# Transposing two row tiles of a fused attention and expert kernel by DMA instead of TensorE, and adding a constant row by VectorE instead of by DMA

## The chip, the cores and the metric

The kernel runs on the 8 cores of one Trainium2 chip. Each core works on one sequence of 4096 rows by 1024 columns and talks to no other core. The metric is the device time of the slowest core, in microseconds. Before the change it is 1058.75 us (median of 3 runs, 1055.48 to 1062.07).

Each core has engines that run their own instruction streams and meet at semaphores: TensorE (PE, matmul), VectorE (DVE), ScalarE (ACT), GpSimd (POOL), and SyncE (SP), which here only issues DMA. POOL issues DMA too, through another queue; both queues share 16 DMA engines.

## The reference, cut to what matters

```python
# per core: x [4096, 1024]; 16 heads of 64; chunks of 128 rows
q, k, v = phi(x @ Wq.T + bq), phi(x @ Wk.T + bk), x @ Wv.T + bv     # phi = elu + 1
for each chunk i:                                     # per head, state S, z carried along
    scores = tril(q_i @ k_i.T)
    out_i  = (scores @ v_i + q_i @ S) / sum(q_i * (cumsum(k_i) + z))
    S, z   = S + k_i.T @ v_i, z + sum(k_i)
x = layernorm(x + out @ Wo.T + bo)
gates = softmax(x @ gate_w.T + gate_b); top 2 of 8 experts per row
x = layernorm(x + sum over the two of gate * (x @ expert_w[e].T + expert_b[e]))
```

## The kernel before

The first stage (about 50 to 650 us) goes over the sequence in 32 chunks of 128 rows; the second (from about 655 us) over 39 tiles of rows sorted by expert, twice. The change touches the first stage only.

Every engine's stream is written out in program order; an engine runs its own rows strictly in that order and stops at the first wait that isn't met. One pass g of the chunk loop writes, in this order, work on three or four chunks at once:

- the norm of chunk g-2 (`stage_ln`, two ACT instructions), writing `x1b` (bf16 rows) and `xf` (f32 rows), and the top-2 gating of chunk g-3 (`stage_top2`, eight small DVE instructions, the sixth of which gives the one-hot tile `oh`);
- chunk g's key transposes and scores on PE (`stage_kt`, `stage_scores`). DVE copies the keys out of PSUM (L417) and masks the scores in two halves (L438);
- one "unit" (`nxt()`), which is 8 matmuls of 128x512 for the projections of the next 512 columns of the sequence. A query or key unit is drained by two ACT instructions (L325, L326) and one DVE instruction (L330), a value unit by one ACT instruction (L339). Then the rank matmuls of chunk g-3 (`stage_rank`, L656 and L658), which wait for `oh`;
- `stage_attnT(g - 1)`: 8 PE transposes of the attention rows `attn` into PSUM (L529) and an ACT copy to `attnT` (L535); a unit; `stage_x1T(g - 2)`: the same for `x1b` into `x1T` (L593, L599);
- `stage_numden(g)`: 24 small matmuls (L461, L467). Those of a half need that half of the masked scores. DVE divides and writes `attn` (L479, L483);
- a unit, the state update (`stage_state`), the output projection of chunk g-1 (`stage_oproj`, L547, from `attnT`), whose DVE part adds the residual rows `x0b` (L554) and takes the norm's statistics; a unit; the gate matmuls of chunk g-2 (`stage_gate`, L609, from `x1T`); two more units.

A pass has six units once the first four chunks are through. In passes 4n to 4n+2 the last two are key or query units, so DVE's last instruction of the pass is L330; in passes 4n+3 the last two are value units and DVE has nothing of them. Units stop with pass 30; passes 28 to 31 have few.

The residual rows plus a constant row `cbc` (bo plus bv times Wo) are made by DMA alone: SP copies `cbc` into `x0b(g)` inside SBUF (`preset_x0`), and POOL then issues a DMA of x with `accum_op=add` onto it (`add_x0`). `x0b(g)` is free again when chunk g-2's L554 is done. `cbc` itself is made in pass 0 by `make_c` (c_tok).

## Time and profile before

| | |
|---|---|
| median of 3 runs | 1058.75 us (1055.48 to 1062.07) |
| profiled execution, its own time | 1057.53 us |
| its span on the slowest core (core 6) | 1056.0 us; the other cores 1041.1 to 1051.1 |
| busy over the span | PE 908.1 us (86%), DVE 576.9 (55%), ACT 540.7 (51%), POOL 431.5 (41%) |
| middle of the chunk loop, 101.9 to 594.8 us (492.9 us) | PE 462.4 us, DVE 331.7, ACT 312.4, POOL 191.3 |
| DMA, share of 16 engines | POOL's queue 54.9%, SP's queue 26.3% |

The last but one line is the middle of the chunk loop, from pass 2 to pass 29. Busy time alone says that PE is nearest to full there, at 94%. What ends its idle time is read from the timeline of single passes, whose period is 17.3 to 19.0 us. Times in a timeline are those of the start; an instruction's duration overlaps the next one's start by 0.05 to 0.1 us on DVE and by more on PE, so what an instruction adds is best read as the difference of two starts.

### The profile page before, as it was taken

How to read it: one execution, taken by the hardware profiler on the slowest of the kernel's cores; microseconds unless marked ns; L12 is line 12 of the kernel's file. 1: busy time of each engine (PE TensorE's matmuls, PEld its weight loads, DVE VectorE, ACT ScalarE, POOL GpSimd, SP SyncE). 2: the span in 40 equal slices, each digit the busy share in tenths (PEclk: the TensorE clock that was granted, in tenths of full speed). 3: DMA queues.
4: the chain of work that ended last, by engine and by line, in shares of the span. 5: the costliest groups of instructions: out<-in, count | busy, mean ns of one | idle time of the engine just before them, and what ended most of it. 6: DMA issues, size and time to landing. Idle time of an engine off the chain costs nothing.

```text
span 1056.0 us, 21222 instructions; the slowest of 8 cores (1041.1 to 1056.0 us)
## 1 busy us (share of the span) xinstructions
PE 908.1 (86%) x6495; PEld 457.0 (43%) x6606; DVE 576.9 (55%) x1243; ACT 540.7 (51%) x731; POOL 431.5 (41%) x674
## 2 busy tenths in 40 slices
PE   4799899999998999999999863579778899999992
PEld 1344454555544545554555541234333344444441
DVE  4345766766666667666667764000000088888883
ACT  0663665756657566566656541112112455666552
POOL 9101433534434334325232424313222356777763
PEclk9899999999999999999999986889989899999997
DMA  9989796977976967868537995989999768987861
GB/s 139 160 156 314 138 209 143 177 156 149 180 155 130 189 150 137 189 126 157 137 106 226 285 294 180 296 160 235 182 168 255 203 210 277 309 267 249 304 208 58
DMA packets 126490, 204.96 MB, mean 194 GB/s; under 512 B 59422, under 2 KB 73886, under 8 KB 126384
## 3 DMA queue, kind: packets, MB, share of 16 engines
q0 software_dynamic: 53808, 130.92, 54.9%
q1 hardware_dynamic: 72576, 72.69, 26.3%
q8 instruction: 59, 0.97, 0.4%
q14 instruction: 47, 0.39, 0.1%
HBM read 142.93 MB, written 97.21 MB: 227 GB/s over the span
## 4 chain that ended last, share of the span: by engine, by line
PE 52%; ACT 11%; issue 10%; DMA 8%; POOL 7%; DVE 7%; SPq 3%; DVEq 0%; ACTq 0%; POOLq 0%
PE PS L309 20%; PE PS L960 13%; PE PS L547 10%; ACT AR L325 4%; DMA AR<-xs 4%; POOL out L206 3%; ACT AR L326 3%; DMA W<-wq 2%; SPq L983 2%; PE PS L467 1%; PE PS L593 1%; PE PS L461 1%; POOL rstd L1126 1%; DMA y2d<-AR,ix 1%; PE PS L502 1%
## 5 line engine op out<-in xcount | busy, mean ns | idle before, releaser
L309 PE MATMUL PS<-W 128*128 128x512 bf16 x1474 | 347.9, 384 | 33.6 <-DVE acc L266 15.0
L960 PE MATMUL PS<-W,AR 128*128 (+1 forms) x1215 | 285.3, 391 | 46.1 <-DMA AR<-xs 40.3
L309 PEld LDWEIGHTS PS<-W 128*128 128x128 bf16 x1536 | 143.7, 99 | 192.4 <-issue 38.4
L960 PEld LDWEIGHTS PS<-W,AR 128*128 128x128 bf16 x1248 | 121.6, 100 | 208.3 <-issue 80.8
L330 DVE SCALAR_TENSOR_TENSOR W<-AR 128x512 bf16<-128x512 f32 x128 | 88.5, 692 | 140.6 <-ACT AR L326 125.3
L325 ACT ACTIVATE AR<-PS,cbs 128x512 f32<-128x512 f32 x128 | 87.9, 687 | 87.8 <-PE PS L309 82.6
L547 PE MATMUL PS<-W 128*128 128x512 bf16 x496 | 115.2, 386 | 6.5 <-DVE ixf L637 3.2
L1022 ACT ACTIVATE AR<-PS 128x1024 f32<-128x1024 f32 x39 | 39.8, 1023 | 152.2 <-PE PS L960 147.3
L1066 DVE COPY wT<-PS 16x128 bf16<-16x128 bf16 x39 | 7.3, 188 | 186.5 <-PE PS L1058 186.0
L206 POOL DMA_INDIRECT xs<-AR x32 | 34.5, 1078 | 181.4 <-DVE rden L479 143.0
L1096 ACT ACTIVATE AR<-AR,nmr,rstd 128x1024 f32<-128x1024 f32 x39 | 48.4, 1241 | 80.4 <-POOL nmr L1129 80.4
L206 POOL DMA_INDIRECT y2d<-AR,ix x39 | 37.6, 963 | 125.0 <-ACT AR L1022 110.4
L326 ACT ACTIVATE AR<-PS,cbs 128x512 f32<-128x512 f32 x128 | 87.7, 685 | 0.0
L438 DVE TENSOR_TENSOR W<-PS,cbs 128x1024 bf16<-128x1024 f32 x64 | 75.1, 1215 | 0.1
L547 PEld LDWEIGHTS PS<-W 128*128 128x128 bf16 x512 | 48.3, 99 | 60.6 <-issue 8.1
L518 ACT ACTIVATE AR<-S_f 64x520 bf16<-64x520 f32 x62 | 39.8, 642 | 51.1 <-DVE S_f L509 46.6
L206 POOL DMA_INDIRECT out<-AR x39 | 53.1, 1360 | 30.2 <-issue 9.9
L565 POOL TENSOR_TENSOR rstd<-mnv,epst 128x1 f32<-128x1 f32 x32 | 6.2, 194 | 137.5 <-DVE mnv L563 120.4
L1111 DVE SCALAR_TENSOR_TENSOR AR<-PS,AR 128x1024 f32<-128x1024 f32 x39 | 50.1, 1284 | 21.3 <-PE PS L960 20.9
L402 POOL DMA_DIRECT2D AR<-x x32 | 32.3, 1046 | 67.6 <-DMA AR<-AR 67.3
L1117 DVE BATCH_NORM_STATS2 lnst<-AR 128x6 f32<-128x512 f32 x78 | 50.2, 685 | 6.5 <-DVE AR L1111 6.2
L1107 DVE SCALAR_TENSOR_TENSOR AR<-AR 128x1024 f32<-128x1024 f32 x39 | 50.1, 1285 | 4.7 <-DMA AR<-y2d,AR 3.6
(123 smaller groups left out, 1265.4 us busy)
## 6 DMA issues: line engine op xcount, KB each, us to landing
AR<-xfd SPq DMA_DIRECT2D x39, 524.0 KB
AR<-AR SPq DMA_DIRECT2D x32, 512.0 KB, 5.8
AR<-x POOLq DMA_DIRECT2D x32, 512.0 KB, 7.2
escr<-ew POOLq DMA_DIRECT2D x64, 256.0 KB
W<-escr SPq DMA_DIRECT2D x40, 256.0 KB, 5.1
W<-xt POOLq DMA_DIRECT2D x64, 128.0 KB, 12.7
W<-escr SPq DMA_DIRECT2D x48, 128.0 KB
xfd<-AR SPq DMA_DIRECT2D x9, 524.0 KB, 6.2
```

The source lines that it names most:

```text
L206: return Q.op("POOL", lambda e: e.indirect_dma_start(out=out, out_offset=bass.IndirectOffsetOnAxis(ap=idx, axis=0), in_=in_, in_offset=Non ...
L309: return Q.op("PE", lambda e: e.matmul(bank(b), lt, rh, start=(k == 0), stop=(k == KB - 1)), inc="cpe" if k == KB - 1 else None)
L325: Q.op("ACT", lambda e: e.activation(e1, bank(b), AF.Exp, bias=bc), inc="cac")
L326: va = Q.op("ACT", lambda e: e.activation(e2, bank(b), AF.Relu, bias=bc), inc="cac")
L330: vd = Q.op("DVE", lambda e: e.scalar_tensor_tensor(dst, e1, 1.0, e2, ALU.min, ALU.add), inc="cdv")
L438: msc_tok[j][hf] = Q.op("DVE", lambda e, hf=hf: e.tensor_tensor(msc[j][hf].rearrange("p (h w) -> p h w", w=128), PS[:, hf * 1024:(hf + 1) ...
L547: vpe = Q.op("PE", lambda e, b=b, k=k, hh=hh: e.matmul(bank(b), attnT[j][:, k * 128:(k + 1) * 128], wcol(3, k, hh * 512, 512), start=(k == ...
L960: mm = e.matmul(bank(2 * pi + hh), xTb[i][:, k * 128:(k + 1) * 128], w, start=(lst == 1 and k == 0), stop=(k == KB - 1))
L1096: vo = Q.op("ACT", lambda e, x=x, val=val: e.activation(val, val, AF.Identity, bias=nmr[x][:, 0:1], scale=rstd[x][:, 0:1]), inc="cac")
L1107: v1 = Q.op("DVE", lambda e, i=i, j=j, val=val: e.scalar_tensor_tensor(val, Y[j], XF[i][:, F_GATE + 1:F_GATE + 2], val, ALU.mult, ALU.add) ...
L1111: v2 = Q.op("DVE", lambda e, i=i, pi=pi, val=val: e.scalar_tensor_tensor(val, PS[:, pi * 1024:(pi + 1) * 1024], XF[i][:, F_GATE:F_GATE + 1 ...
L1117: vb = Q.op("DVE", lambda e, i=i, x=x, hh=hh: e.bn_stats(lnst[x][:, hh * 6:(hh + 1) * 6], XF[i][:, hh * 512:(hh + 1) * 512]), inc="cdv")
```

## The change

Two independent edits.

First, for the first 24 chunks the 8 PE transposes of `attn` and their ACT copy are left out, and so are those of `x1b`; in their place SP issues one DMA transpose each, from SBUF to SBUF (`move_attnT(g)` after `stage_numden(g)`, `move_x1T(g - 2)` after `stage_ln(g - 2)`). Chunks 24 to 31 keep the PE form.

Second, for all 32 chunks SP loads x plainly into `x0b` (`load_x0`), and DVE adds `cbc` with one 128x1024 f32 instruction (`add_c(g)`) at the end of pass g. The copy of `cbc` and POOL's accumulating DMA are gone.

```diff
+    def load_x0(g):
+        Q.wait("SP", *(et_free if own(g) else [x0_free[g % 2]]))
+        x0_tok[g] = dma("SP", f"dx{g % 2 + 2 * own(g)}", x0b(g),
+                        dx[g * 128:(g + 1) * 128, :])
+
+    def add_c(g):
+
+        Q.wait("DVE", x0_tok[g], c_tok[0])
+        x0_add[g] = Q.op("DVE", lambda e: e.tensor_tensor(x0b(g), x0b(g), cbc, ALU.add),
+                         inc="cdv")
+
+
+    moved = lambda g: g < NCH - 8
+
+    def turn(sem, out, in_):
+        return Q.op("SP", lambda e: e.dma_start_transpose(
+            out.rearrange("p (k m) -> p k m", m=128), in_), inc=sem, k=16)
+
+    def move_attnT(g):
+        j = g % 2
+        Q.wait("SP", attn_tok[j], attnT_free[j])
+        attnT_tok[j] = attn_free[j] = turn(f"dat{j}", attnT[j], attn[j])
+
+    def move_x1T(g):
+        x, j = g % 3, g % 2
+        Q.wait("SP", x1b_tok[g], x1T_free[j])
+        x1T_tok[g] = turn(f"dxT{j}", x1T[j], x1b[x][:, 0:1024])
+        x1b_free[x] = [x1T_tok[g]]
...
             stage_ln(g - 2)
+            if moved(g - 2):
+                move_x1T(g - 2)
             stage_meta(g - 2)
...
-        if on(1) and g < NCH:
+        if on(1) and g < NCH and not moved(g - 1):
             stage_attnT(g - 1)
         nxt()
         if late:
             nxt()
-        if on(2):
+        if on(2) and not moved(g - 2):
             stage_x1T(g - 2)
...
-        if on(0) and g > 0 and not own(g):
-            add_x0(g)
-        if g == NCH - 4:
-            add_x0(NCH - 2)
-            add_x0(NCH - 1)
         if on(0):
             stage_numden(g)
+            if moved(g):
+                move_attnT(g)
...
         if g == 0:
-            preset_x0(0)
-            add_x0(0)
+            load_x0(0)
+        if on(0):
+            add_c(g)
         if g + 1 < NCH - 2:
-            preset_x0(g + 1)
+            load_x0(g + 1)
         if g == NCH - 5:
-            preset_x0(NCH - 2)
-            preset_x0(NCH - 1)
+            load_x0(NCH - 2)
+            load_x0(NCH - 1)
```

On DVE, the end of a pass whose last units are query or key units and the top of the next pass read so before (L330 drains the units, L629 to L646 are the gating, L417 and L438 the copy of the keys and the mask):

```order
106 L330 SCALAR_TENSOR_TENSOR W<-AR 128x512 x2
107 L629 RECIPROCAL rg<-sg 128x1
108 L630 MAX t<-eg 128x8
109 L632 MAX_INDEX ix<-t,eg 128x8
110 L633 TENSOR_SCALAR AR<-t,rg 128x2
111 L637 CAST ixf<-ix 128x2
112 L639 TENSOR_TENSOR oh<-cbs,ixf 128x16
113 L646 TENSOR_TENSOR AR<-oh,t 128x16
114 L417 COPY AR<-PS 128x1024
115 L438 TENSOR_TENSOR W<-PS,cbs 128x1024 x2
```

In the changed kernel, whose lines are numbered 18 higher from there on, the same place reads:

```order
110 L330 SCALAR_TENSOR_TENSOR W<-AR 128x512 x2
111 L403 TENSOR_TENSOR AR<-AR 128x1024
112 L647 RECIPROCAL rg<-sg 128x1
113 L648 MAX t<-eg 128x8
114 L650 MAX_INDEX ix<-t,eg 128x8
115 L651 TENSOR_SCALAR AR<-t,rg 128x2
116 L655 CAST ixf<-ix 128x2
117 L657 TENSOR_TENSOR oh<-cbs,ixf 128x16
118 L664 TENSOR_TENSOR AR<-oh,t 128x16
119 L435 COPY AR<-PS 128x1024
120 L456 TENSOR_TENSOR W<-PS,cbs 128x1024 x2
```

The new row L403 stands between the drain of the last unit and the gating; everything behind it is in its old order.

On PE, between the gate matmuls of one pass and the first matmuls of the next pass's `stage_numden`, the rows were:

```order
224 L609 MATMUL PS<-gw_b,AR 128x8 x8
225 L309 MATMUL PS<-W 128x512 x16
226 L412 MATMUL PS<-id_b,W 128x128 x8
227 L433 MATMUL PS<-W 128x128 x16
228 L309 MATMUL PS<-W 128x512 x8
229 L656 MATMUL PS<-oh,stri_b 128x16
230 L658 MATMUL PS<-acc,ones_b 128x16
231 L529 MATMUL PS<-id_b,W 128x128 x8
232 L309 MATMUL PS<-W 128x512 x8
233 L593 MATMUL PS<-id_b,AR 128x128 x8
234 L461 MATMUL PS<-AR,W 128x130
```

and are now:

```order
209 L627 MATMUL PS<-gw_b,AR 128x8 x8
210 L309 MATMUL PS<-W 128x512 x16
211 L430 MATMUL PS<-id_b,W 128x128 x8
212 L451 MATMUL PS<-W 128x128 x16
213 L309 MATMUL PS<-W 128x512 x8
214 L674 MATMUL PS<-oh,stri_b 128x16
215 L676 MATMUL PS<-acc,ones_b 128x16
216 L309 MATMUL PS<-W 128x512 x8
217 L479 MATMUL PS<-AR,W 128x130
```

Both sets of 8 transposes (L529, L593) stood between the scores and `stage_numden`, and both are gone from there; nothing else on PE has moved.

## Rows read from the trace of the kernel before

**Rows 1.** Page, part 2: busy tenths of PE in 40 slices of the span
```profile
PE   4799899999998999999999863579778899999992
```
**Rows 2.** Stretches: us, busy (count) of PE, PEld, DVE, ACT, POOL; PEclk, DMA share, GB/s
```profile
101.90:594.80 492.90, 462.39 (x4057) 252.85 (x4122) 331.67 (x806) 312.39 (x473) 191.29 (x333) 1.00 0.76 163
198.60:215.90 17.30, 17.09 (x152) 9.42 (x154) 9.66 (x28) 10.17 (x16) 8.25 (x14) 1.00 1.00 188
```
**Rows 3.** Timeline, top of pass 10: start us, us, engine line operation [idle before <-releaser]
```profile
242.65 0.30 ACT L622 ACTIVATE eg<-lg,ngm 128x8 f32<-128x8 f32 x1 [1.23 <-DVE ngm L619]
245.22 1.25 ACT L579 ACTIVATE AR<-AR,nmr,rstd 128x1024 bf16<-128x1024 f32 x1
245.45 0.69 DVE L330 SCALAR_TENSOR_TENSOR W<-AR 128x512 bf16<-128x512 f32 x1 [0.47 <-ACT AR L326]
246.06 0.16 DVE L629 RECIPROCAL rg<-sg 128x1 f32<-128x1 f32 x1
247.32 0.17 PE L656 MATMUL PS<-oh,stri_b 128*128 128x16 bf16 x1 [0.78 <-DVE oh L639]
247.39 0.69 DVE L417 COPY AR<-PS 128x1024 bf16<-128x1024 bf16 x1
247.99 2.35 DVE L438 TENSOR_TENSOR W<-PS,cbs 128x1024 bf16<-128x1024 f32 x2
248.22 1.89 PE L309 MATMUL PS<-W 128*128 128x512 bf16 x8 [0.17 <-DVE AR L417]
249.95 0.61 PE L593 MATMUL PS<-id_b,AR 128*128 128x128 bf16 x8
250.39 0.22 PE L461 MATMUL PS<-AR,W 128*128 128x130 bf16 x1
251.56 1.67 PE L309 MATMUL PS<-W 128*128 128x512 bf16 x7
253.38 0.69 ACT L325 ACTIVATE AR<-PS,cbs 128x512 f32<-128x512 f32 x1 [1.67 <-PE PS L309]
258.73 0.34 PE L609 MATMUL PS<-gw_b,AR 128*128 128x8 bf16 x8
```
**Rows 4.** Timeline, top of pass 12, behind value units
```profile
280.08 0.16 DVE L619 TENSOR_REDUCE ngm<-lg 128x1 f32<-128x8 f32 x1
281.19 0.16 DVE L629 RECIPROCAL rg<-sg 128x1 f32<-128x1 f32 x1 [0.96 <-ACT eg L622]
283.14 2.35 DVE L438 TENSOR_TENSOR W<-PS,cbs 128x1024 bf16<-128x1024 f32 x2
286.28 0.61 PE L593 MATMUL PS<-id_b,AR 128*128 128x128 bf16 x8
```
**Rows 5.** Page, part 5: the nearest row to the new addition
```profile
L1107 DVE SCALAR_TENSOR_TENSOR AR<-AR 128x1024 f32<-128x1024 f32 x39 | 50.1, 1285 | 4.7 <-DMA AR<-y2d,AR 3.6
```
**Rows 6.** Timeline and chain of work that ended last, passes 0 to 2
```profile
83.71 1.19 SPq L194 DMA_DIRECT2D xfd<-AR  x1
...
85.42 6.64 DMA AR<-AR
...
87.74 0.69 DVE L330 SCALAR_TENSOR_TENSOR W<-AR 128x512 bf16<-128x512 f32 x1 [2.39 <-ACT AR L326]
88.35 0.68 DVE L417 COPY AR<-PS 128x1024 bf16<-128x1024 bf16 x1
...
100.88 0.69 DVE L554 TENSOR_TENSOR AR<-PS,AR 128x512 f32<-128x512 f32 x1 [4.09 <-DMA AR<-x]
101.93 1.67 PE L309 MATMUL PS<-W 128*128 128x512 bf16 x7 [1.31 <-DVE AR L554]
107.33 0.61 PE L593 MATMUL PS<-id_b,AR 128*128 128x128 bf16 x8 [1.56 <-ACT AR L579]
```
**Rows 7.** One line's instructions: count, duration ns min/median/max; and a stretch of the second stage
```profile
L983 SPq DMA_TRANSPOSE AR<-xs x39: 1237/1464/13554, 651.7 to 823.9; - x39
...
800.00:830.00 30.00, 29.89 (x137) 13.62 (x139) 0.00 (x0) 9.21 (x9) 9.63 (x10) 1.00 1.02 256
```
**Rows 8.** Timeline, top of pass 30
```profile
603.75 0.16 DVE L629 RECIPROCAL rg<-sg 128x1 f32<-128x1 f32 x1 [0.59 <-ACT eg L622]
```

More of the change, by code:

```diff
@@ L379, in build @@
     rden_tok = [None, None]
-    x0_set, x0_free = {}, [None, None]
+    x0_tok, x0_free = {}, [None, None]
     x0_add = {}
@@ L393, in build @@
     x0b = lambda g: tmp[:, g % 2 * 1024:(g % 2 + 1) * 1024] if own(g) else x0c[g % 2]
-    def preset_x0(g):
-        Q.wait("SP", *(et_free if own(g) else [x0_free[g % 2]]), c_tok[0])
-        x0_set[g] = dma("SP", f"dc{g % 2 + 2 * own(g)}", x0b(g), cbc)
-    def add_x0(g):
-        Q.wait("POOL", x0_set[g])
-        x0_add[g] = Q.op("POOL", lambda e: e.dma_start(
-            x0b(g), dx[g * 128:(g + 1) * 128, :], accum_op=ALU.add),
-            inc=f"dx{g % 2 + 2 * own(g)}", k=16)
+    def load_x0(g):
[19 more added lines that the diff above has]
+        x1b_free[x] = [x1T_tok[g]]
     def stage_kt(g):
```

## The prediction

> **What bounds the kernel now.** I read the page's busy slices first, then the stretches of the chunk loop, then the timeline of single passes. The slices show PE at eight tenths or more from the third to the 23rd slice [rows 1], and the middle of the chunk loop has PE busy 462.4 of 492.9 us, DVE 331.7, at full clock, with the DMA engines at 0.76 [rows 2]. So 30.5 us of PE time are idle there over some 27 passes. That looks like a loop bound by PE, from which any PE work taken out would be gained. The timeline says that this is only half true. At the top of pass 10 [rows 3] two chains run side by side from the pass before to `stage_numden`. PE's own: units, key transposes, scores, unit, rank, attnT, unit, x1T, numden. And one over ACT and DVE: the gating's exponential (L622) waits for DVE and delays the draining of the last units on ACT; DVE then drains the last unit (L330 at 245.45), runs the gating (from 246.06), copies the keys (247.39) and masks the scores (247.99, 2.35 us, done 250.34). PE waits for that chain twice, 0.78 us for `oh` before L656 and 0.17 us for the bank that L417 frees, and starts numden at 250.39, 0.05 us after the masks are done. The two chains are equally long; what is taken from PE alone between them gains little, and what is put on DVE there costs. Behind value units (pass 12, [rows 4]) DVE is ahead instead: it stands idle 0.96 us before L629, and its masks are done at 285.49, 1.24 us before numden (286.73, below). Passes with index 4n+1, 4n+2 and 4n+3 have the first form, passes 4n the second.
>
> **The change part by part.**
>
> *PE transposes out.* A set of 8 occupies PE from 249.95 to 250.39, 0.44 us [rows 3]. 24 sets of each kind are left out: 48 x 0.44 = 21 us is the most that PE alone could give back. The ACT copies go too, but behind them ACT stands idle waiting for PE before its next unit (1.67 us before 253.38, [rows 3]), so I cost them at nothing; what hides them is the next unit's matmuls.
>
> *The addition in.* No row has an f32 sum of two 128x1024 SBUF tiles. The nearest has the same size, type and two SBUF operands and takes 1.285 us [rows 5]; the masks, with one operand in PSUM, take 2.35 us for two. From those a start-to-start cost of 1.13 to 1.28 us; I take 1.15, since L438 starts follow each other about 1.13 apart. It is placed behind L330 and ahead of L629, so the whole gating, the key copy and the masks are queued behind it, and PE waits for `oh` and for the masks.
>
> *Pass of the first form, redone with both edits (pass 10).* L330 ends its turn at 246.06; the addition holds DVE to 247.21; `oh` and so L656 move from 247.32 to 248.47. The unit behind it no longer needs the transposes' bank and starts at 248.54, runs 1.73 (248.22 to 249.95, [rows 3]) to 250.27. The masks are done at 250.34 + 1.15 = 251.49, the first half near 250.36. numden's first half runs 250.45 to 250.9, its second must wait for 251.49, starts at 251.6 and ends at 252.05. Before, the unit behind numden started at 251.56 less its missing first record, about 251.35. **+0.72 us per pass**, although PE has 0.9 us less to do: PE now stands idle about 1.9 us for `oh` and 0.7 us for the second mask.
>
> *Pass of the second form (pass 12).* The addition starts at 280.2 in DVE's idle time and ends at 281.35, 0.15 us later than L629 started [rows 4]. The masks stay ahead of PE. Both sets of transposes are gained, 2 x 0.44, and the short wait at the scores with them: **-0.9 us**; numden began at 286.28 + 0.45 = 286.73 and would begin at 285.85.
>
> *Sum over the loop.* Both kinds are out in passes 4 to 24: 15 passes of the first form, 15 x 0.72 = +10.8, and 6 of the second, 6 x -0.9 = -5.4. Together +5.4 us.
>
> *Passes 25 to 31.* Pass 25 has one set back, +0.9. Passes 26 and 27 have both sets back and the addition, up to +1.0 each. In passes 28 to 31 DVE waits 0.59 us for ACT before L629 [rows 8], so 1.15 - 0.59 = 0.56 us is left: four times, 2.2. In all +5 us at most; I take 4.2, since pass 28 comes behind value units.
>
> *The start.* Before, the sum of x and the constant for chunk 0 was late: the copy was issued at 85.42 and took 6.64 us, the accumulating DMA came behind it, DVE waited 4.09 us at L554 and PE 1.31 and 1.56 us behind it [rows 6]. Now the load is issued behind SP's init rows (until 84.90) and the new transpose of chunk 0 (about 1.3 us, the issue time of the second stage's transposes, [rows 7]), so at 86.2, and if it takes the same 6.64 us it lands at 92.9. DVE comes to the addition at 88.35 and stops there, and behind it in its queue stand L417 (then at 88.35) and pass 1's masks, for which PE's numden of pass 1 waits. Masks and numden are late by 92.9 + 1.15 - 88.35 = 5.7 us; 2.87 us of PE waits that followed are gone. **+3 us** (0 if the load is quick, +5.7 if those waits stay).
>
> *The transposes by DMA.* Those of the second stage, from HBM, are 39, of the same 128x1024 bf16; SP spends 1.46 us on one at the median, and from 800 to 830, where PE has 137 matmuls, 16 to a tile, so a tile in 3.5 us, it is busy 29.89 of 30 us [rows 7]. So one costs at most 3.5 us of throughput. From SBUF none is in the trace; between 1.3 and 3.5 us is my bound if the source makes no difference. What hides them: `x1T` can be issued when L579 is done (246.47) and is needed at 258.73 [rows 3], 12.3 us; `attnT` has a whole pass, about 17. SP has two of them and a load in a pass of 18.6 us. In DMA time one copy and an accumulation of 512 KB go, a plain load of 512 KB and two transposes come: about 0.76 to 0.85 of the engines. I cost them at nothing. Without cover, each us that `x1T` is late costs a us.
>
> *POOL* loses 32 DMA issues of 1 us, and waits elsewhere: nothing.
>
> *Sum.* +5.4 + 4.2 + 3 = +12.6 us on the profiled execution's 1057.53 us (its span 1056.0 and 1.5 around it), 1070.1. The median of the runs is 1.2 us above that execution: **1071 us**.
>
> **The rivals.**
>
> *Faster.* The one way is that the addition finds a gap. The point from which it decides is DVE's cost of the addition: at 0.55 us or less a first-form pass gains nothing or better, and at zero the second half of numden starts right at 250.34 + 0.1 and ends at 250.9, -0.43 per pass. That gives 15 x -0.43 - 5.4 = -12, with the start at 0 to +3: 1047 to 1050. For it speaks that busy time has PE at 94%, and that ACT, freed of 2 us per pass, might drain earlier than I think; against it that DVE's L330 waits only 0.47 us before the addition's place and that ACT's delay there comes from L622, not from the copies. Chance 0.17.
>
> *x1T late.* Behind pass 4n+2 POOL issues eight loads of xt and three casts right before `x1T` is ready, and the stretch there has the DMA engines at 1.00 [rows 2]. A transpose shares the rings with them. If it takes over 12.3 us there, PE waits at the gate matmuls. Two us late in those six passes gives +12, 1083; one us in all 24, +24, 1095. For it: the longest issue of a transpose in the second stage, 13.55 us, behind other traffic [rows 7]. Against: PE lived with 1.02 of DMA share in 800:830 without a wait. Chance 0.2.
>
> *The transposes fill the queue.* If one from SBUF takes more than 18.6 / 2 = 9.3 us, two per pass are more than the pass. At the 13.55 us of the longest, 27.1 - 18.6 = 8.5 us per pass, 24 times: +204, far off. The 3.5 us speaks against it. Chance 0.05.
>
> A rule stands beside this one. The Trainium skill, page "VectorE: DVE Perf Modes", section "The three transpose paths", has 390 ns for a 128x128 block on TensorE and 1309 ns by DMA, and its rules say to use TensorE where PSUM will do, which speaks against the change. Eight blocks in a row would be an estimated 10.5 us by that page, two of them 21 us per pass, and the sum 2.4 x 24 = 58 us above the present time. The second stage's at most 3.5 us for eight blocks doesn't agree with taking them in a row; no run here shows it from SBUF.
>
> *Nothing moves*, gains and losses of the passes cancel at 1055 to 1062. Chance 0.08.
>
> **How the numbers follow.** My forecast has 0.5, own range 1062 to 1079: the addition at 1.13 to 1.28, the start 0 to 5.7, the late passes 2 to 5. Late x1T 0.2, full queue 0.05, faster 0.17, nothing 0.08. The range from 1049 to 1092 leaves out most of the full queue, a fifth of the late x1T, and half of the faster case. About 1% is what a measurement of this kernel can tell from no change, 1048 to 1069. Slower than that: 0.32 of my forecast, 0.2 and 0.05: 0.57. Within: 0.18, the 0.08 and 0.03 of the faster case: 0.29. Faster: 0.14.
>
> **What would show it.** Right: in first-form passes PE's wait before the rank matmuls (`oh`) grows from 0.8 to near 1.9 us, and a new wait for the masks of 0.5 to 0.8 us stands inside numden; periods of 19.4 us there and 16.5 in the fourth; no wait of PE for a DMA at the output projection or the gate; DVE idle before the first addition for about 4.6 us. Wrong: the addition far from 1.15 us; waits of the gate matmuls for `x1T`; or a DVE chain that has moved ahead as a whole, with all passes near 17.5 us.

## The result, and the profile after

The median of 4 runs of the changed kernel is 1095.5 us (1088.35 to 1104.58). Kernel before, run beside it on the same chip: 1058.75 us (3 runs, 1055.48 to 1062.07). A fourth took 1072.17 us (the median of all four is 1060.41), in a slower state that comes over some runs of every kernel here, and such runs are left out of all medians and ratios below. The ratio is 1.0356, 95% interval 1.0311 to 1.0402: 37 us slower, where 12 were forecast.

```profile
span 1103.0 us, 20614 instructions; the slowest of 8 cores (1073.1 to 1103.0 us)
PE 924.3 (84%) x6222; PEld 444.0 (40%) x6222; DVE 613.5 (56%) x1275; ACT 499.2 (45%) x683; POOL 412.0 (37%) x642
...
PE   4697888988998999989899986439899799999993
...
PEclk9888999889999999999999998679999989999997
...
q1 hardware_dynamic: 123264, 85.28, 36.3%
```

This is the page of the changed kernel, whose profiled execution is its slowest (1104.58 us, core 1 ends last). PE has 48 sets of 8 matmuls fewer to do, yet is busy 16 us longer than before (908.1). Its slices fall from nines to eights and nines over the whole loop, against [rows 1]. The granted clock has eights in slices 8 and 9 (193 to 248 us), in the middle of the loop. POOL has a new wait of 225.7 us in all, on the transposes of the norm rows. SP's queue (q1), which issues the transposes, has 36.3% of the DMA time where it had 26.3.

Stretches, columns as in [rows 2], the changed kernel, core 1 and then core 6:

```profile
101.90:594.80 492.90, 439.33 (x3458) 222.01 (x3456) 333.05 (x758) 246.93 (x390) 158.14 (x285) 0.95 0.81 144
```
```profile
146.10:223.80 77.70, 69.73 (x545) 35.52 (x554) 54.88 (x127) 40.83 (x66) 28.27 (x48) 0.96 0.83 156
301.50:377.30 75.80, 67.03 (x546) 34.37 (x553) 53.84 (x125) 40.19 (x64) 26.11 (x48) 1.00 0.79 153
377.30:533.50 156.20, 142.09 (x1089) 75.02 (x1104) 107.07 (x245) 80.02 (x128) 51.90 (x94) 0.93 0.83 151
```

In the stretch of [rows 2] PE is busy 439.3 us where it had 462.4, since fewer passes fit into it, and the clock is 0.95 where it was 1.00. The three stretches of core 6 hold 4, 4 and 8 passes: 77.7, 75.8 and 78.1 us for four. Only the one with the clock at 1.00 is near the forecast.

What PE and POOL wait for in the changed kernel, core 1 (us in all, times, longest):

```profile
POOL AR L701 <- DMA AR<-AR: 225.7, 24, 15.4
...
PE PS L674 <- DVE oh L657: 38.5, 21, 2.5
...
PE PS L627 <- DMA AR<-AR: 13.2, 7, 3.5
```

L674 is the rank's first matmul (L656 before), L627 the gate's (L609 before). The second row was forecast. The third was the sign under "Wrong".

**Where the time went.** For every kernel I took the start of `stage_numden`'s first matmul (L461 before, L479 after) in each pass, 32 starts on a core; a period "to pass n" runs from that of pass n-1 to that of pass n. Three sums in us:

| kernel, core | to passes 1 to 4 | 5 to 24 | 25 to 31 | all |
|---|---|---|---|---|
| before, 1 | 61.5 | 370.6 | 110.6 | 542.7 |
| before, 6 | 60.9 | 370.5 | 110.6 | 542.0 |
| changed, 1 | 67.8 | 401.0 | 119.1 | 588.0 |
| changed, 6 | 65.8 | 387.4 | 120.6 | 573.9 |

What lies ahead of pass 0 and behind pass 31 differs from core to core and run to run by more than between the two kernels (behind: 425.9 and 436.2 us before, 433.2 and 418.9 after), so the loss is in these passes: 32 us on core 6, 45 on core 1 (of the slowest cores of the two kernels, 46). The runs' median, +37, lies between. The profiled execution, the slowest of its four, stands near the upper end.

### The profile page after: what moved, and what is told of

It reads as the page before. It is cut to its first block, busy times and chain, and to the rows that moved or that the text cites. A ratio compares the mean times of both kernels' runs of the same rounds, so it can differ in the third digit from the quotient of the medians.

```text
span 1103.0 us, 20614 instructions; the slowest of 8 cores (1073.1 to 1103.0 us)
## 1 busy us (share of the span) xinstructions
PE 924.3 (84%) x6222; PEld 444.0 (40%) x6222; DVE 613.5 (56%) x1275; ACT 499.2 (45%) x683; POOL 412.0 (37%) x642
## 3 DMA queue, kind: packets, MB, share of 16 engines
q1 hardware_dynamic: 123264, 85.28, 36.3%
## 4 chain that ended last, share of the span: by engine, by line
PE 37%; DMA 17%; issue 11%; POOL 10%; SPq 8%; DVE 8%; ACT 7%; DVEq 0%; POOLq 0%; ACTq 0%
PE PS L309 18%; PE PS L565 8%; DMA AR<-AR 8%; PE PS L978 5%; DMA AR<-xs 3%; SPq L1001 3%; POOL out L206 3%; ACT AR L325 2%; DMA W<-xt 2%; POOL AR L212 2%; DVE W L456 2%; SPq L194 2%; DVE AR L403 2%; ACT AR L326 2%; POOL rstd L1144 2%
## 5 line engine op out<-in xcount | busy, mean ns | idle before, releaser
L309 PE MATMUL PS<-W 128*128 128x512 bf16 x1536 | 378.3, 398 | 24.5 <-DVE acc L266 15.0
L309 PEld LDWEIGHTS PS<-W 128*128 128x128 bf16 x1536 | 147.4, 101 | 199.4 <-issue 58.4
L330 DVE SCALAR_TENSOR_TENSOR W<-AR 128x512 bf16<-128x512 f32 x128 | 88.6, 692 | 161.2 <-ACT AR L326 159.7
L565 PE MATMUL PS<-W 128*128 128x512 bf16 x512 | 118.8, 386 | 3.8 <-ACT W L553 3.2
L1040 ACT ACTIVATE AR<-PS 128x1024 f32<-128x1024 f32 x39 | 39.8, 1024 | 147.8 <-PE PS L978 122.3
L701 POOL COPY AR<-tok_i 128x1 int32<-128x1 int32 x32 | 6.0, 187 | 225.7 <-DMA AR<-AR 225.7
L565 PEld LDWEIGHTS PS<-W 128*128 128x128 bf16 x512 | 48.2, 99 | 60.4 <-issue 8.0
L583 POOL TENSOR_TENSOR rstd<-mnv,epst 128x1 f32<-128x1 f32 x32 | 7.0, 220 | 164.0 <-DVE mnv L581 144.3
L206 POOL DMA_INDIRECT out<-AR x39 | 52.2, 1338 | 27.1 <-issue 16.5
L206 POOL DMA_INDIRECT xs<-AR x32 | 36.4, 1137 | 69.0 <-DVE rden L497 25.8
L339 ACT ACTIVATE AR<-PS 128x512 bf16<-128x512 f32 x64 | 37.3, 592 | 53.4 <-PE PS L309 52.0
```

The source lines that it names most:

```text
L206: return Q.op("POOL", lambda e: e.indirect_dma_start(out=out, out_offset=bass.IndirectOffsetOnAxis(ap=idx, axis=0), in_=in_, in_offset=Non ...
L309: return Q.op("PE", lambda e: e.matmul(bank(b), lt, rh, start=(k == 0), stop=(k == KB - 1)), inc="cpe" if k == KB - 1 else None)
L330: vd = Q.op("DVE", lambda e: e.scalar_tensor_tensor(dst, e1, 1.0, e2, ALU.min, ALU.add), inc="cdv")
L565: vpe = Q.op("PE", lambda e, b=b, k=k, hh=hh: e.matmul(bank(b), attnT[j][:, k * 128:(k + 1) * 128], wcol(3, k, hh * 512, 512), start=(k == ...
```

## What the changed kernel's timeline shows

**The chain of DVE, as forecast.** Top of pass 9, changed kernel, core 1, columns as in [rows 3]:

```profile
253.15 1.22 DVE L403 TENSOR_TENSOR AR<-AR 128x1024 f32<-128x1024 f32 x1
...
254.29 0.16 DVE L647 RECIPROCAL rg<-sg 128x1 f32<-128x1 f32 x1
...
255.55 0.17 PE L674 MATMUL PS<-oh,stri_b 128*128 128x16 bf16 x1 [1.92 <-DVE oh L657]
...
255.68 1.89 PE L309 MATMUL PS<-W 128*128 128x512 bf16 x8
...
258.71 0.22 PE L479 MATMUL PS<-AR,W 128*128 128x130 bf16 x1 [0.50 <-DVE acc L679]
```

L403 is the addition. It holds DVE from 253.15 to 254.29, 1.14 us, and PE waits 1.92 us for `oh` where it waited 0.78. The last row is the new wait inside `stage_numden`, 0.50 us; the profile names L679, the short DVE instruction right behind the masks, but what numden's second half needs is the second mask. The next period (to pass 10), which has the same wait and the one for pass 9's second mask, is 19.6 us, 0.8 above the 18.8 of before.

**The clock behind that wait.** Two passes later, the same place and core:

```profile
294.73 0.17 PE L674 MATMUL PS<-oh,stri_b 128*128 128x16 bf16 x1 [1.92 <-DVE oh L657]
...
294.86 3.43 PE L309 MATMUL PS<-W 128*128 128x512 bf16 x8
```

And the stretches there, columns as in [rows 2]:

```profile
296.00:298.00 2.00, 2.00 (x6) 0.71 (x5) 2.00 (x3) 0.00 (x0) 0.00 (x0) 0.50 1.00 141
298.00:301.00 3.00, 3.00 (x33) 1.82 (x31) 1.87 (x8) 1.27 (x2) 0.00 (x0) 0.92 1.30 170
```

The wait is the same 1.92 us, but the unit behind it takes 3.43 us instead of 1.89: the granted clock stands at 0.50, the lower of PE's two levels (1.2 of 2.4 GHz), from 296 to 298. It comes back by itself. On core 1, 10 of the 15 waits of 1.9 to 2.1 us in passes 5 to 27 have a unit of 2.3 us or more behind them, on core 6, 13 of 17. That it is the wait and not the DMA transposes beside it, other kernels show: of the 144 units behind a wait for `oh` in the same passes of all eight cores, 81 are slow here and 37 in e1, which has the long wait and no DMA transposes; e3, which has all the DMA transposes and waits for `oh` of 0.9 us at most, has none. The slow unit runs while DVE makes the second mask, for which PE would have waited anyway, so 1.5 us of it cost a period less than that: the one here (to pass 11) is 20.9 us instead of 19.6, most on core 6 are 20.3.

**x1T late.** Pass 7, changed kernel, core 1:

```profile
210.16 2.43 SPq L410 DMA_TRANSPOSE AR<-AR  x1
...
227.44 0.18 POOL L701 COPY AR<-tok_i 128x1 int32<-128x1 int32 x1 [15.43 <-DMA AR<-AR]
227.46 0.35 PE L627 MATMUL PS<-gw_b,AR 128*128 128x8 bf16 x8 [3.50 <-DMA AR<-AR]
227.67 6.53 PE L309 MATMUL PS<-W 128*128 128x512 bf16 x16
```

The transpose is issued at 210.16 and its landing frees POOL and PE at 227.44: 17.3 us. PE waits 3.50 us, and the clock falls again (granted 0.50 from 227 to 231 us), so the 16 matmuls behind take 6.53 us instead of 3.61. The period (to pass 8) is 24.1 us, 6.6 more than before: the wait is half of the price, the clock behind it most of the other half. In all 24 passes of core 1 the time from issue to landing, with POOL's L701 as the witness, runs from 2.9 us (the last, chunk 23) to 17.3, and it goes by the pass: passes 7, 11, 15, 19 and 23 have 17.3, 16.0, 13.8, 10.6 and 14.9, passes 6, 10, 14, 18 and 22 have 5.9, 5.5, 5.6, 8.2 and 6.0. Passes 4n+3 are those in which POOL has issued eight loads of xt just before. Pass 20 stands apart, with 12.8 us and a gate wait of 1.87 us. Core 6 has 9.2 to 13.1 us in passes 7, 11, 15, 19 and 23, 3.8 to 5.6 in passes 4n+2, and no wait at the gate; the other cores have 1.3 to 11.5 us of gate waits in all, core 1 13.2.

**x1T issued late, by POOL's wait.** Pass 3 to pass 4, changed kernel, core 1:

```profile
143.10 0.21 DVE L581 BATCH_NORM_AGGREGATE mnv<-lnst 128x2 f32<-128x12 f32 x1
144.15 0.18 POOL L701 COPY AR<-tok_i 128x1 int32<-128x1 int32 x1 [8.55 <-DMA AR<-AR]
148.46 0.21 POOL L583 TENSOR_TENSOR rstd<-mnv,epst 128x1 f32<-128x1 f32 x1
151.29 1.42 SPq L410 DMA_TRANSPOSE AR<-AR  x1
162.35 0.35 PE L627 MATMUL PS<-gw_b,AR 128*128 128x8 bf16 x8 [3.41 <-DMA AR<-AR]
```

The statistics of chunk 2 are there at 143.31, but POOL, which makes the norm's factors from them (L583), stands at L701 until the transpose of the chunk before has landed, and then has two scatters to issue. So L583 starts 5.1 us late, and the norm and its transpose with it. The transpose lands 10.9 us after its issue, less than the slack of 12.3, and PE waits 3.41 us all the same. Issued 5.1 us earlier and as quick it would have landed at 157.1, ahead of PE, which stood from 158.94 (an estimate from these rows). On core 1, L583 starts 1.4 to 6.4 us behind its statistics in ten chunks, on core 6 1.4 to 3.0 us in seven, and in the kernel before never more than 0.2 us on either.

## The experiments

Twelve kernels, four to a chip, each compared with the kernel before on the same chip. Diffs are against the changed kernel where nothing else is said. The table has the periods of core 1 (others where named); the median of the kernel before was 1053.69 us for the first four, 1056.56 for the next four, 1054.09 for the last four. The ratios are formed from the runs and can differ by some 0.3% from the quotient of the medians.

| kernel | median us | ratio (95%) | passes 1 to 4 | 5 to 24 | 25 to 31 |
|---|---|---|---|---|---|
| e1 addition alone | 1088.92 | 1.0322 (1.0278 to 1.0367) | 67.1 | 395.1 | 117.8 |
| e2 DMA transposes alone | 1083.15, 1092.17 | none | 59.7 | 405.2 | 111.1 |
| e3 both, addition moved | 1065.89 | 1.0124 (1.0073 to 1.0175) | 55.5 | 385.3 | 114.2 |
| e4 filling before the rank | 1103.47 | 1.0470 (1.0418 to 1.0521) | 69.0 | 395.7 | 119.0 |
| e5 addition moved, alone | 1054.32 | 1.0013 (0.9971 to 1.0055) | 57.6 | 372.4 | 113.9 |
| e6 e3 with x1T on PE | 1056.58 | 0.9981 (0.9940 to 1.0021) | 55.7 | 374.0 | 112.2 |
| e7 e3, xt loads later | 1082.29 | 1.0244 (1.0167 to 1.0321) | 55.6 | 396.3 | 114.3 |
| e8 half an addition | 1076.07 | none | 66.0 | 381.8 | 114.8 |
| e9 DVE order, on before | 1041.01 | 0.9888 (0.9852 to 0.9925) | 61.8 | 360.2 | 108.9 |
| e10 e9 and e11 together | 1039.71, 1044.75 | none | 58.4 | 365.1 | 111.0 |
| e11 e6 from chunk 6 | 1052.77 | 0.9982 (0.9959 to 1.0005) | 58.4 | 365.6 | 113.2 |
| e12 e7, bookkeeping first | 1090.03 | 1.0332 (1.0292 to 1.0373) | 55.7 | 408.0 | 117.7 |

For e2, e8 and e10 one or two single runs stand in place of a median, and no ratio was formed, so their times are less sure than the others.

**e1: the addition alone.** Both transposes back on PE.

```diff
-    moved = lambda g: g < NCH - 8
+    moved = lambda g: False
```

> Only the second edit: plain load of x and the VectorE addition at the end of each pass; all transposes stay on TensorE. Theory 1 (the addition lengthens the DVE chain L330, gating, key copy, masks, which PE waits for, and PE's longer wait for oh, 0.78 + 1.15 = 1.9 us, drops the granted clock): first-form passes 19.8 to 20.6 us instead of 18.8, granted clock 0.93 to 0.97 in the loop, start +5, late passes +4, so 1085 to 1100 us, nearly all of the loss of the full change (+35). Rival (the DMA transposes are the cost): within 15 us of before, 1060 to 1075, clock 1.00 in the loop.

35 us above the kernel before. Periods in passes of the first form are 20.0 us (before 18.8: the addition whole) and 21.3 to 21.6 in five; the second form keeps its 17.5. Top of passes 10 and 11, core 1:

```profile
260.95 0.17 PE L674 MATMUL PS<-oh,stri_b 128*128 128x16 bf16 x1 [1.92 <-DVE oh L657]
...
261.85 1.46 PE L309 MATMUL PS<-W 128*128 128x512 bf16 x6 [0.17 <-DVE AR L435]
```
```profile
280.93 0.17 PE L674 MATMUL PS<-oh,stri_b 128*128 128x16 bf16 x1 [1.92 <-DVE oh L657]
...
281.82 2.72 PE L309 MATMUL PS<-W 128*128 128x512 bf16 x6
```

The first six matmuls of the unit take 1.46 us behind one wait of 1.92 us and 2.72 behind the next of the same length. 5 of 19 such waits on this core (one of them 2.3 us long) are followed by a slow unit. No DMA is waited for in the loop here, so the clock falls without the DMA transposes too. The start has its +5.6 us. The interval of e1 (1.0278 to 1.0367) overlaps that of the changed kernel (1.0311 to 1.0402): with the addition where it is, taking the DMA transposes back out gains nothing that these runs can tell.

**e2: the DMA transposes alone.** The residual is preset and accumulated by DMA as before (`preset_x0`, `add_x0`), and the moves stay:

```diff
+        if on(0) and g > 0 and not own(g):
+            add_x0(g)
...
         if g == 0:
-            load_x0(0)
-        if on(0):
-            add_c(g)
+            preset_x0(0)
+            add_x0(0)
         if g + 1 < NCH - 2:
-            load_x0(g + 1)
+            preset_x0(g + 1)
```

> Only the first edit: DMA transposes in the first 24 chunks; the constant row stays with the SBUF copy and the accumulating DMA. Theory 1: first-form passes lose 0.4 us each (18.4), second-form passes 0.9 (16.6), the loop -12 us; the late x1T of passes 4n+3 (2 to 3.5 us of wait at the gate matmuls, and half clock behind it) costs 2 to 6 us in some of six passes, so 1048 to 1070 us. Rival (the DMA transposes are the cost): 1080 us or more.

1083.15 and 1092.17 us, 29 and 38 above the kernel before. So the rival came: the transposes, forecast at nothing, cost as much as the addition, beside the preset copy and the accumulating DMA that e2 keeps. Beside plain loads (e3, below) they cost 12 us. Periods of the first form are 18.5, shorter than before, so PE does gain from the missing work; the loss is in single passes: 33.5 us to pass 5, 24.3, 27.4 and 23.2 to later ones. What PE waits for, core 1:

```profile
PE PS L673 <- DVE oh L656: 17.8, 20, 2.5
PE PS L626 <- DMA AR<-AR: 16.0, 6, 4.6
PE PS L564 <- DMA W<-W: 15.1, 2, 7.9
```

6 gate waits and 2 waits at the output projection (for attnT), none of which the kernel before has. The two parts of the change are not additive: +35 and about +34 alone, +37 together. PE, held up by the addition, comes later to the gate, and its waits there are shorter: 0 to 13.2 us in all on a core in the changed kernel, 3.2 to 22.0 in e3 and 16.0 to 43.5 in e2. How much of the difference this makes is not shown.

**e3: addition moved behind `stage_numden`.** There DVE has no one waiting; chunk 0's is done in pass 1.

```diff
             if moved(g):
                 move_attnT(g)
+            if g == 1:
+                add_c(0)
+            if g > 0:
+                add_c(g)
...
-        if on(0):
-            add_c(g)
```

> The full change, but the addition is put into DVE's stream behind the division of stage_numden, where DVE is idle 0.6 to 1.5 us in each pass, instead of at the pass's end; chunk 0's is done in pass 1. Theory 1: PE's wait for oh is back at 0.8 us or less, clock 0.99 to 1.00 except behind a late x1T, the 5 us of the start are gone: 1045 to 1070 us. Rival (any 1.15 us more on DVE costs the same, or the DMA transposes are the cost): 1085 us or more.

12 us above the kernel before instead of 37. The start is shorter than before (55.5 against 61.5), the first form is 18.5. What is left are passes with a late transpose: core 1 has 27.5, 25.6 and 21.6 us to passes 5, 8 and 12, core 4 (the slowest) 25.7, 23.8, 23.3, 24.3 and 24.2 to passes 5, 8, 12, 16 and 20. PE's gate waits: 10.7 us in 5 on core 1, 22.0 in 7 on core 4.

**e4: PE work put into the wait.** The changed kernel, with attn still transposed on PE as filling before the rank, its result thrown away. It asks whether the clock could be held.

```diff
             nxt()
+            if on(3) and moved(g - 1):
+                fill(g - 1)
             if on(3):
                 stage_rank(g - 3)
```

> The full change, and in passes 3 to 24 the eight attn transposes are kept on PE ahead of the rank matmuls as filling, their result unused (more work, not less). Theory: PE's idle time before the rank matmuls falls from 1.92 to about 1.5 us; if the half clock behind that wait is set off by the length of the idle time, first-form passes go from 20.3 to 19.6 us and the kernel gains 5 to 12 us on the full change (1083 to 1090). Rival (the clock falls all the same, or isn't what costs): 1095 us or up to 10 more.

It did not help: 1103.47 us. Top of pass 6, core 1:

```profile
186.56 0.61 PE L675 MATMUL PS<-id_b,W 128*128 128x128 bf16 x8
188.65 0.17 PE L688 MATMUL PS<-oh,stri_b 128*128 128x16 bf16 x1 [1.48 <-DVE oh L657]
...
189.55 3.54 PE L309 MATMUL PS<-W 128*128 128x512 bf16 x8 [0.70 <-DVE AR L435]
```

The wait for `oh` shrinks to 1.48, but the filling takes a bank that the key copy (L435) then frees late, and a second wait of 0.70 stands behind it; the unit takes 3.54 us all the same. Whether a filling that needs no bank would hold the clock stays open.

**e5: the addition moved, no DMA transposes.** e1 and e3's edits together:

```diff
-    moved = lambda g: g < NCH - 8
+    moved = lambda g: False
...
+            if g == 1:
+                add_c(0)
+            if g > 0:
+                add_c(g)
...
-        if on(0):
-            add_c(g)
```

> Plain load and VectorE addition, the addition behind the division of stage_numden as in e3, all transposes on TensorE. Theory (the cost of e1 is the place of the addition, not its 1.15 us of DVE time): first-form passes back at 18.8 us, second 17.5, start 5 us shorter than before, so 1045 to 1054 us, 0 to 10 us under before. Rival (DVE time itself costs): 1070 us or more.

The same as the kernel before: 1.0013. Start 57.6 (4 us gained), middle 372.4 against 370.6, late passes 113.9 against 110.6. So e1's 35 us came from the place of the addition, none from the operation. The start, core 1:

```profile
90.60 2.35 DVE L456 TENSOR_TENSOR W<-PS,cbs 128x1024 bf16<-128x1024 f32 x2
...
95.50 2.35 DVE L403 TENSOR_TENSOR AR<-AR 128x1024 f32<-128x1024 f32 x2
```

The key copy and masks run as soon as DVE is free of L330 and the two additions (chunks 0 and 1) come behind them, waiting for nothing.

**e6: e3 with x1T back on PE.** attnT is the only DMA transpose left.

```diff
-            if moved(g - 2):
-                move_x1T(g - 2)
...
-        if on(2) and not moved(g - 2):
+        if on(2):
             stage_x1T(g - 2)
```

> As e3, but only the attention rows go by DMA, the norm rows' transposes stay on PE. Theory (the late one is x1T, needed 12 us after it is ready, while attnT has 17): no wait at the gate matmuls, first-form passes 18.4 to 18.8, second 17.0, 1035 to 1050 us. Rival (any DMA transpose comes late behind the loads of xt): PE waits for attnT at the output projection, 1060 us or more.

Ratio 0.9981, as fast as before, and slower than the 1035 to 1050 us expected; no core has a gate wait for a DMA. The step from e3 to e6 is what the x1T transposes cost: 385.3 against 374.0 us in passes 5 to 24 on core 1. Its periods are 18.5, 18.5, 17.4 and 18.1 (72.5 for four, before 74.0), but the one to pass 5 has 29.5. There the attnT of chunk 3 is late. It was issued behind eight loads of xt and three casts:

```profile
125.95 2.03 SPq L410 DMA_TRANSPOSE W<-W  x1
...
147.53 4.85 PE L565 MATMUL PS<-W 128*128 128x512 bf16 x11 [8.55 <-DMA W<-W]
```

It is issued at 125.95 and lands 21.3 us later, more than the 17 us of slack, and PE waits 8.55 us for it at the output projection of pass 4, again with slow matmuls behind (4.85 us for 11, at a granted clock of 0.52). SP needs 6.76 us to issue the next one, at 138.77. Every core has one such wait, of 0.3 to 9.7 us.

**e7: xt loads half a pass later.** e3, with `load_xt` behind the `stage_numden` of passes 4n+3 instead of at the end of 4n+2. If the loads make x1T late, the late one must move to passes 4n.

```diff
+            if c == 3 and s + 2 < NSC:
+                load_xt(s + 2, [unit_done[(s, 23)]])
...
-        if on(0) and c == 2 and s + 2 < NSC:
-            load_xt(s + 2, [unit_done[(s, 23)]])
```

> As e3, but POOL issues the eight loads of xt half a pass later, behind stage_numden of the pass with index 4n+3 instead of at the end of pass 4n+2, so behind that pass's transpose of x1b. Theory (the loads of xt on the other queue make x1T late): the waits of 3 to 4 us at the gate matmuls of passes 4n+3 fall to under 1 us, period behind them 17 to 18 instead of 23 us, 1040 to 1055 us against e3's 1066. Rival (the transposes are slow by themselves or behind the casts): waits stay, 1060 us or more.

Issue, landing of x1T (L701) and xt loads, core 1, passes 7 and 8:

```profile
202.54 1.23 SPq L410 DMA_TRANSPOSE AR<-AR  x1
...
207.21 0.18 POOL L701 COPY AR<-tok_i 128x1 int32<-128x1 int32 x1 [7.10 <-DMA AR<-AR]
...
211.73 4.35 POOL L194 DMA_DIRECT2D W<-xt  x8
...
220.02 2.11 SPq L410 DMA_TRANSPOSE AR<-AR  x1
...
228.62 3.57 PE L309 MATMUL PS<-W 128*128 128x512 bf16 x8 [5.00 <-DMA W<-xt]
232.69 0.18 POOL L701 COPY AR<-tok_i 128x1 int32<-128x1 int32 x1 [12.88 <-DMA AR<-AR]
```

In pass 7 the same transpose now lands after 4.7 us (17.3 in the changed kernel), in pass 8 after 12.7 (9.4). The gate waits are gone and the periods to passes 4n are 17.2 to 17.3. That shows the cause of the late ones in passes 4n+3. It is no cure, and the 1040 to 1055 us expected did not come: the units now wait for xt itself, 38.1 us in 7 waits on core 1 (6.8 in one in the kernel before), and the kernel is slower than e3 (ratio 1.0244 against 1.0124).

**e8: half an addition.** e1 with 512 of the 1024 columns added; the other half of the constant is left out of the result.

```diff
-        x0_add[g] = Q.op("DVE", lambda e: e.tensor_tensor(x0b(g), x0b(g), cbc, ALU.add),
+        x0_add[g] = Q.op("DVE", lambda e: e.tensor_tensor(
+            x0b(g)[:, 0:512], x0b(g)[:, 0:512], cbc[:, 0:512], ALU.add),
                          inc="cdv")
...
-    moved = lambda g: g < NCH - 8
+    moved = lambda g: False
```

> e1 with only columns 0 to 511 of the constant row added (the other half of the addition is left out). Theory (time goes with the DVE chain, and the clock falls once PE's idle time before the rank matmuls is long enough): the wait for oh is 1.3 to 1.4 us instead of 1.92, first-form passes 19.3 us at granted clock 1.00 and without the 21 us passes, 1068 to 1078 us, half or less of e1's loss. Rival (the loss is the wait for the load or the start): 1083 us or more.

1076.07 us in its one run, 20 above the kernel before. The periods are very regular: 19.4 to 19.5 in the first form (18.8, 19.4, 20.0 for none, half, all of the addition), 17.5 in the second. The wait, core 1:

```profile
256.84 0.17 PE L675 MATMUL PS<-oh,stri_b 128*128 128x16 bf16 x1 [1.41 <-DVE oh L658]
...
257.74 1.46 PE L309 MATMUL PS<-W 128*128 128x512 bf16 x6 [0.17 <-DVE AR L436]
```

Of 19 waits on this core (18 of about 1.4 us, one of 1.76) one has a slow unit behind it, against 5 of 19 at 1.92 us in e1 and none of 18 at 0.8 to 1.2 in the kernel before. In passes 5 to 24 the half costs 11.2 us and the whole 24.5: the second half costs 13.3, more than the first, since it brings more of the lower clock.

**e9: the kernel before, with DVE's order changed.** The key copy and the masks ahead of the gating, rank and scatter behind `stage_numden`, in passes 3 to 27. It asks what the chain is worth. Diff against the kernel before:

```diff
-        if on(3):
+        first = on(3) and not (on(0) and not late)
+        if first:
             stage_top2(g - 3)
...
             stage_scores(g)
+        if on(3) and not first:
+            stage_top2(g - 3)
...
             stage_numden(g)
+            if on(3) and not first:
+                stage_rank(g - 3)
+                stage_scatter(g - 3)
```

> The kernel before with only the order changed: in passes 3 to 27 DVE copies the keys and masks the scores ahead of the gating of chunk g-3, and the rank matmuls and the scatter of that chunk come behind stage_numden. Theory (in first-form passes DVE's chain L330, gating, copy, masks is as long as PE's, and PE waits for it): PE's wait of 0.8 us for oh goes, first-form periods 17.8 to 18.0 instead of 18.8, second 17.3 to 17.5, the loop 14 to 20 us shorter, 1036 to 1044 us. Rival (PE's work sets the period and the waits are made up elsewhere): 1052 to 1062 us.

Ratio 0.9888, interval 0.9852 to 0.9925: this one beats both kernels. Top of a pass, core 1:

```profile
263.18 0.68 DVE L417 COPY AR<-PS 128x1024 bf16<-128x1024 bf16 x1
...
263.77 2.35 DVE L438 TENSOR_TENSOR W<-PS,cbs 128x1024 bf16<-128x1024 f32 x2
263.93 1.89 PE L309 MATMUL PS<-W 128*128 128x512 bf16 x8
...
266.04 0.15 DVE L629 RECIPROCAL rg<-sg 128x1 f32<-128x1 f32 x1
...
267.30 0.17 PE L656 MATMUL PS<-oh,stri_b 128*128 128x16 bf16 x1
```

Same DVE work, but the rank's matmul, now behind numden, has no wait, and four passes take 72.0 us instead of 74.0. In passes 5 to 24 that is 10.4 us. The first form gains 1.0 to 1.4 us a pass, but the period to passes 4n rises from 17.5 to 18.9: there PE now waits 1.05 us at the output projection for DVE's part of the rank (L665), which the new order puts later. So the order is not free, and the 14 to 20 us expected for the loop came to 10.4.

**e11: e6, with attnT by DMA only from chunk 6.**

```diff
-    moved = lambda g: g < NCH - 8
+    moved = lambda g: 6 <= g < NCH - 8
```

(with e6's edits)

> e6 with the DMA transposes starting at chunk 6 instead of 0. Theory (e6's pass 5, 28 us long, is its transpose behind the early traffic of the rings): pass 5 back at 18.8 us, 1045 to 1052 us. Rival (the wait moves to the first pass with a transpose): 1055 us or more.

The period to pass 5 is 18.9 and passes 5 to 24 of core 1 take 365.6 us, 5 less than before. Yet the median is the same as before's (0.9982), above the 1045 to 1052 us expected: core 3, the slowest, has one of 25.8 us (to pass 21), with a wait of 5.50 us for attnT. So the early transposes were the trouble of the period to pass 5; the attn transposes taken off PE are worth 5.0 and 7.5 us in passes 5 to 24 on two cores without such a wait (core 1, core 6), and one late transpose takes that away.

**e10: e9's order on top of e11.**

```diff
-    moved = lambda g: g < NCH - 8
+    moved = lambda g: 6 <= g < NCH - 8
...
+        if on(3) and not first:
+            stage_top2(g - 3)
...
             stage_numden(g)
+            if on(3) and not first:
+                stage_rank(g - 3)
+                stage_scatter(g - 3)
```

(with e6's edits)

> e9's order, plain load and VectorE addition behind the division of stage_numden, and the attention rows' transposes by DMA for chunks 6 to 23 only. Theory: with DVE's chain out of the way the 0.44 us of PE transposes are gained whole in every pass, first form 17.4 to 17.6, second 16.9 to 17.1, the start 4 us shorter: 1022 to 1036 us. Rival (DVE, fuller by the addition, is again the limit): same as e9 or up to 10 us above it.

1039.71 and 1044.75 us. Core 6 has 357.8 us in passes 5 to 24 (e9: 360.2), core 1 one pass of 24.9. Not to be told from e9; the 1022 to 1036 us expected did not come.

**e12: e7 with `stage_meta` ahead of `move_x1T`.** POOL's L701 writes a word of the norm rows' tile behind the transposed columns, so `x1b_free` makes it wait for the transpose's landing, 225.7 us in all. If that holds up the xt loads, e7's waits for xt should go.

```diff
             stage_ln(g - 2)
+            stage_meta(g - 2)
             if moved(g - 2):
                 move_x1T(g - 2)
-            stage_meta(g - 2)
```

(with e7's edits)

> e7 with POOL's index writes into the x1b tile ahead of SP's transpose, so that POOL no longer waits for the transpose to land before it goes on. Theory (e7's loads of xt came late because POOL stood 9 us and more behind the transpose each pass): PE's waits for xt, 20 to 32 us in e7, fall to under 10, 1045 to 1062 us. Rival (the loads of xt are late because they were put later, POOL's wait has no part): waits and time as e7, 1075 to 1085 us.

They did not go: 44.9 us in 7 waits on core 1 (e7: 38.1). So POOL's wait is not what makes the xt loads of e7 late; what is left is that they are issued late. What POOL's wait costs the changed kernel was not measured by a run of its own; the trace shows it in the late issue of pass 4 above.

## Why the prediction was wrong

*The direction and the addition were right.* The addition costs 1.14 us start to start (forecast 1.15), sits where it was put in DVE's queue, and moves `oh` by its length: PE waits 1.92 us (forecast about 1.9). At full clock four passes take 75.7 us on core 6 (passes 13 to 16), 1.6 more than the mean group of before (370.5 / 5 = 74.1); the forecast was 3 x 0.72 - 0.9 = +1.3. e8 and e1 (19.4 and 20.0 us) confirm that the chain passes every tenth of it on.

*Where the difference lies.* The forecast was 3 us for the start, 5.4 for the loop, 4.2 for the late passes and nothing for the transposes by DMA, 12.6 in all. Core 6 has +4.9, +16.9 and +10.0, core 1 +6.3, +30.4 and +8.5.

*The start was under-sized.* The load came 9.7 us behind pass 0's numden on core 1 (forecast 8.4, because the transpose ahead of it took SP 2.32 us and not 1.3) and took 6.7 us (forecast 6.64):

```profile
98.19 1.23 DVE L403 TENSOR_TENSOR AR<-AR 128x1024 f32<-128x1024 f32 x1 [5.73 <-DMA AR<-x]
```

Masks and numden were late by 5.73 + 1.15 = 6.9 us (forecast 5.7), the period to pass 1 rose by 6.2. The 2.87 us of waits behind it [rows 6] did vanish, yet the next two periods gave back only 1.1 us together. The step that failed is again the clock: behind the wait of 5.82 us for the masks (core 6; 6.43 on core 1) the granted clock is 0.50 from 99 to 105 us, numden takes 1.98 us (1.17 in pass 0), and the unit behind it 3.60 instead of 1.89:

```profile
101.15 3.60 PE L309 MATMUL PS<-W 128*128 128x512 bf16 x8
```

e5, which has no such wait, has the period to pass 2 at 13.8 us where before has 17.3 and the changed kernel 16.6. In all +6.3 and +4.9 us against 3; this lay inside my bound for it (5.7) on one core only.

*The loop's term failed in the price of a wait.* I carried DVE's delay forward at PE's full clock: [rows 2] had 1.00 and I took it as given. The change itself lowered it. Against five groups of four at 75.7 us, core 6's 387.4 has 8.9 us more, with the clock at 0.93 to 0.96 there and no gate wait for a DMA. Together with the 8 us of the mechanism that is 16.9 us where 5.4 stood. The late passes are in the main the same error: 10.0 and 8.5 us where 4.2 stood; passes 25 to 27 alone have 20.3, 22.5 and 20.0 us on core 6 (18.8 before), each with a wait for `oh` of 1.9 us. The rest, 3.8 us, is in passes 29 to 31, where e5, with the addition out of the chain, loses 3.1 us too; why is not shown.

*"I cost them at nothing", of the transposes by DMA, is the step that failed outright.* I set the slack of x1T (12.3 us) against the transposes' throughput (3.5 us in the second stage, [rows 7]). What matters is the time from issue to landing, and [rows 7] only tell how often one can be had. Undisturbed, my bound held: the last one took 2.9 us. Behind eight xt loads it took 10.6 to 17.3 on core 1, and above the slack PE waited. Core 1 lost 13.6 us more than core 6 in passes 5 to 24, 12.1 of them in the periods to passes 5 and 8, where its x1T was late and core 6's was not. Of the two, only the one to pass 8 has a transpose slower than its slack; the one to pass 5 has one issued late by POOL. The rival "x1T late" had the place and the cause right for the former (passes behind 4n+2, xt loads on the DMA engines, [rows 2]) and a chance of 0.2. Its 12 us of waits on top of the forecast are near the 13.2 of core 1's gate, though core 6 has none. It took a wait of two us for a loss of two: in pass 7, 3.5 us of wait cost 6.6.

*What the trace of before could have told.* The row for eight xt loads, 1.00 of DMA share over 17.3 us [rows 2], together with SP's longest issue of 13.55 us [rows 7], gave a latency bound of 13 us and more against 12.3 of slack. I weighed it with PE's untroubled second stage, which tests throughput. For attnT I gave 17 us of slack and called it safe; it was late in pass 4 in e2, e3 and e6, in pass 16 in e2 (7.9 us of wait) and in pass 20 in e11.

*The page's rule.* The Trainium skill, page "VectorE: DVE Perf Modes", section "The three transpose paths", would have a tile of eight blocks take an estimated 10.5 us if they go in a row. The 2.9 us of the undisturbed one does not agree with that reading. The advice of that page's section "Rules for kernel authors" to use TensorE for a transpose where PSUM will do as its destination is borne out by the runs: e5, with the transposes on PE, has 1.0013 against the kernel before, e3, with them on DMA, 1.0124.

*The rivals.* "Faster" asked for an addition in a gap: e3 and e5 are that case, and e5 shows it is worth nothing in the loop, only the start's 4 us, which the late passes give back. "The transposes fill the queue" did not come: the mean over 24 passes is near 9 us for x1T on core 1, but SP's next issue does not wait for the landing (issue at 210.16 us, the next one at 218.72, landing at 227.44). POOL's wait I had not seen at all ("waits elsewhere: nothing"). It made the late x1T of pass 4 on core 1; what it costs in all is open.

## What to carry to other kernels

Before an operation is moved to DMA, compare its slack with the longest issue-to-landing time among the traffic that will stand beside it, pass by pass, not with its throughput and not in the mean, and look for who else waits for the landing: a copy on POOL did, and the next chunk's norm stood behind it. When two chains are equally long, look first at the order on the slower engine's queue: the same addition cost 35 us in front of the work that PE waits for and nothing behind it, and reordering DVE without removing anything gained 12 us, more than removing PE work did. Price a new wait of PE with the clock behind it, taken from rows where such a wait already stands.

## What the runs showed of the hardware that I had not expected

- A single wait of PE in a loop that is otherwise full can be followed by half clock. Of the 144 waits for `oh` in passes 5 to 27 of all eight cores, a slow unit follows none in the kernel before (0.8 to 1.2 us long), 8 in e8 (17 of 18 on a core 1.4 us), 37 in e1 (1.9 us) and 81 in the changed kernel (most 1.9 us), where a second wait for the mask follows. Why it is some of equal waits and not all stays open.
- A transpose of 128x1024 bf16 inside SBUF took 2.9 us from issue to landing with little beside it and 10.6 to 17.3 us on core 1 behind eight loads of 128 KB and three of 256 KB (e7: 4.7 in a pass from which those were moved away). One of attnT, of the same size, took 21.3 us in e6 (issued in pass 3, landed in pass 4). SP's issue of one took 1.2 us in quiet places, 6.8 us in pass 4 of e6 and 12.2 us in pass 16 of e2.
- The 48 transposes brought the hardware queue from 72576 packets and 72.69 MB to 123264 and 85.28 MB: 1056 packets of about 250 bytes each. By the queue's share (27.1% of 1086.3 us in e1, 36.3% of 1103.0 in the changed kernel) one occupies all 16 engines for an estimated 2.2 us.
